# The last LayerNorm over two experts, slot matmuls by four experts, and a new order of the first weights, in a decoder layer with 32 experts

## What is computed

```
x = layernorm(x + self_attention(x))       # 16 heads of 64, biases bq, bk, bv, bo
x = layernorm(x + cross_attention(ctx, x)) # one head of 64, masked keys
x = layernorm(x + moe(x)), with
  probs = softmax(x @ gate.T)              # 32 experts
  topw, topi = top_k(probs, 8); topw /= topw.sum(-1)
  # an expert takes at most 512 tokens (CAPACITY), in order of the tokens
  h   = silu(gate_e(x)) * up_e(x)          # 384 wide
  out = sum over the 8 experts of topw * down_e(h)
```

## Time and profile before

| | |
|---|---|
| time, median of 3 runs | 1892.97 us (1891.65, 1892.97, 2359.14) |
| the profiled execution | 1912.09 us, span 1910.4 us, mean granted clock 0.979 |
| busy: PE, PEld, DVE, ACT, POOL | 94%, 54%, 68%, 60%, 34% of the span |
| rounds | to about 1020 us |
| drain and first slots | to about 1096 us, when expert 0 starts |
| experts | to about 1875 us |
| rest | 35 us |
| moved by DMA | 339.27 MB, mean 178 GB/s |

### The profile page before, as it was taken

One profiled execution on the slowest core, in us unless ns is written; L12 is line 12 of the kernel. 1 busy time (PEld: TensorE's weight loads), 2 busy tenths in 40 slices (PEclk: granted clock), 3 DMA queues, 4 the chain that ended last, 5 costly groups with the idle time before them and its releaser, 6 DMA issues.

```text
span 1910.4 us, 40067 instructions
## 1 busy us (share of the span) xinstructions
PE 1804.4 (94%) x13735; PEld 1040.8 (54%) x13735; DVE 1297.7 (68%) x2695; ACT 1148.8 (60%) x2884; POOL 645.9 (34%) x546
## 2 busy tenths in 40 slices
PE   6899999999999999999999799979999999999992
PEld 3566666667666766666665344434444444444440
DVE  5667989898989898989897674424444444444435
ACT  6877988788878887888787333333333333333325
POOL 1111211121211122111211246545655655555542
PEclk8999999999999999999999999989999999999995
DMA  6647655766466646665568399999999999999968
GB/s 204 155 75 131 141 129 107 158 139 145 96 149 149 143 99 143 151 141 108 131 147 179 118 275 189 214 202 237 250 246 235 233 240 239 242 241 246 216 140 321
DMA packets 596821, 339.27 MB, mean 178 GB/s; under 512 B 492704, under 2 KB 523424, under 8 KB 596768
## 3 DMA queue, kind: packets, MB, share of 16 engines
q1 hardware_dynamic: 567760, 267.28, 61.4%
q0 software_dynamic: 29008, 71.32, 17.7%
HBM read 159.72 MB, written 60.29 MB: 115 GB/s over the span
## 4 chain that ended last, share of the span: by engine, by line
PE 34%; SPq 5%; DMA 4%; DVE 3%; ACT 2%; issue 2%; POOL 1%; POOLq 0%; DVEq 0%; ACTq 0%
PE bank L678 22%; PE bank L1134 10%; SPq L517 4%; DMA arena_v<-arena_p 2%; DMA arena_p<-x_rows,cur_from 1%; PE bank L754 1%; DMA out<-arena_p 1%; DMA stage<-acc_rows 1%; POOL arena_p L2373 0%; PE bank L743 0%; DVE stage L1568 0%; SPq L486 0%; ACT arena_p L1554 0%; ACT stage L1554 0%; POOL acc_rows L2378 0%
## 5 line engine op out<-in xcount | busy, mean ns | idle before, releaser
L2300 POOL TENSOR_TENSOR arena_q<-arena_q 128x512 f16<-128x512 f32 x128 | 166.7, 1303 | 828.7 <-ACT arena_q L1205 721.2
L1568 DVE SCALAR_TENSOR_TENSOR arena_wo<-stage,arena_wo 128x3072 f16<-128x3072 f32 (+3 forms) x78 | 182.4, 2342 | 288.3 <-ACT arena_wo L1313 253.9
L678 PE MATMUL bank<-xt,arena_wo 128*128 128x256 f16 x3072 | 361.4, 275 | 13.1 <-DVE arena_wo L1568 6.9
L678 PEld LDWEIGHTS bank<-xt,arena_wo 128*128 128x128 f16 x3072 | 296.2, 98 | 73.0 <-issue 18.3
L2378 POOL DMA_INDIRECT acc_rows<-arena_wo,cur_to x124 | 203.3, 1639 | 249.6 <-ACT arena_wo L1539 231.3
L678 PE MATMUL bank<-arena_v,arena_wo 128*128 128x512 f16 x1152 | 256.6, 384 | 17.7 <-DMA arena_v<-arena_p 14.6
L1134 PE MATMUL bank<-arena_wo 128*128 128x512 f16 x1152 | 258.2, 383 | 5.4 <-DVE arena_wo L2254 4.6
L678 PE MATMUL bank<-arena_q,arena_wo 128*128 128x512 f16 x1152 | 251.2, 379 | 1.0 <-issue 1.0
L1224 ACT ACTIVATE arena_p<-bank,s_neg 128x256 f32<-128x256 f32 x508 | 234.3, 481 | 29.6 <-DVE s_neg L1604 27.8
L1205 ACT ACTIVATE arena_q<-bank,bqkv 128x256 f32<-128x256 f32 (+1 forms) x512 | 201.7, 485 | 82.4 <-PE bank L678 82.1
L1568 DVE SCALAR_TENSOR_TENSOR stage<-arena_p,s_rden,stage 128x256 f16<-128x256 f32 x508 | 211.7, 478 | 28.3 <-ACT stage L1245 28.3
(11 more groups left out here) (272 smaller groups left out, 2274.1 us busy)
## 6 DMA issues: line engine op xcount, KB each, us to landing
stage<-wguT SPq DMA_DIRECT2D x31, 1536.0 KB
stage<-wdnT SPq DMA_DIRECT2D x32, 768.0 KB, 5.8
xt<-xT SPq DMA_DIRECT2D x16, 512.0 KB, 4.8
xr<-x_rows SPq DMA_DIRECT2D x16, 512.0 KB, 4.1
stage<-ctxT SPq DMA_DIRECT2D x16, 512.0 KB, 3.8
acc_rows<-x SPq DMA_DIRECT2D x15, 512.0 KB, 3.0
x_rows<-stage SPq DMA_DIRECT2D x30, 256.0 KB, 3.7
arena_p<-stage SPq DMA_TRANSPOSE x256, 3.1
```

Of the source, the lines that this page charges most:

```text
L678: mm = pe.matmul(out_ap, lhs(a, i), rhs(c, i), start=(n == 0 and i == 0), stop=(n == 2 and i == chunks - 1))
L1568: return vec.scalar_tensor_tensor(out=dst, in0=src, scalar=scale, in1=hi, op0=ALU.mult, op1=ALU.subtract)
L2300: gp.tensor_tensor(qk[:, j % 2, 1, :], qk32[:, j % 2, :], qk[:, j % 2, 0, :], ALU.subtract).then_inc(qk_lo, 1)
```

## The change

It has four parts.

- **Slots.** In rounds 3 to 15 `fill_slots` uses the form of `fill_rest`: 16 matmuls of 128 x 128 by 128 x 64 for a batch in the place of 64. `add_slots` adds 128 x 512 in the place of 32 x 512. Three small copies on VectorE in the drain (`own_slots`) bring the diagonal blocks together. `bias_rows` has memory of its own, and the index tables move into memory of the context's.
- **Weights in round 0.** `Q2` and `K2` are loaded and split before `V1`. `Q2` takes the place of `K0`, `V1` that of `V0`.
- **First expert.** SP starts the load of expert 1's weights after the first gate product of expert 0, and VectorE does `rest_hots(0)` before its two copies.
- **The last LayerNorm.** The groups are loaded when the scatters of experts 0 to 29 have landed, and their moments, deviations and normalising stand between the steps of experts 30 and 31. Expert 30 isn't scaled on ScalarE or scattered with an addition: GpSimd gathers its rows from `acc_rows`, VectorE adds its result (`fix_sums(0)`), and GpSimd writes the rows back to `acc_rows` after all groups are loaded. Then it gathers expert 31's rows and goes on as before with both sets: over `out`, first those of expert 30, then those of expert 31. TensorE's last `down` waits for `fix_sums(0)`. The memory of the groups is assigned in another order. The last two experts stand outside TensorE's loop.

The diff, cut to its core:

```
-                 [quad(stage[:, 0, 0:GT_ROWS])], [quad(stage[:, 0, GT_ROWS:2 * GT_ROWS])],
-                 [quad(arena_p[:, 0:GT_ROWS])], [quad(arena_v[:, :].bitcast(F32))],
+                 [quad(arena_p[:, 0:GT_ROWS])], [quad(arena_p[:, CC * (D + NX):CC * (D + NX) + GT_ROWS])],
                  [pair_of(x1h[:, :, :].rearrange("p s n -> p (s n)").bitcast(F32)),
                   pair_of(x1T[:, :, :, :, :].rearrange("p s t c n -> p (s t c n)").bitcast(F32))],
-                 [quad(arena_p[:, CC * (D + NX):CC * (D + NX) + GT_ROWS])]]
+                 [quad(stage[:, 0, 0:GT_ROWS])], [quad(stage[:, 0, GT_ROWS:2 * GT_ROWS])],
+                 [quad(arena_v[:, :].bitcast(F32))]]
...
+        LATER = NX - 2
+        fix = [[y[:, 0, c, :] for c in range(CC)], [x1[:, 0, :], x1[:, 1, :], x2[:, 0, :], x2[:, 1, :]]]
...
-        AT = {Q0: 0, K0: 1024, V0: 2048, Q1: 4096, K1: 5120, V1: 0, Q2: 2048, K2: 4096, O0: 0, O1: 2048, X3: 4096, XO: 6144}
-        AFTER = {V1: K0, Q2: V0, K2: K1, O0: V1, O1: Q2, X3: K2}
+        AT = {Q0: 0, K0: 1024, V0: 2048, Q1: 4096, K1: 5120, Q2: 0, V1: 2048, K2: 4096, O0: 0, O1: 2048, X3: 4096, XO: 6144}
+        AFTER = {Q2: K0, V1: V0, K2: K1, O0: Q2, O1: V1, X3: K2}
...
-            for n in (V0, Q1, K1, V1, Q2, K2):
+            for n in (V0, Q1, K1, Q2, K2, V1):
...
-            for c in range(CC):
-                sp.wait_ge(ld_first[c], 16)
             sp.wait_ge(ew_lo_gu, 1)
             sp.wait_ge(ew_lo_dn, 1)
+            sp.wait_ge(g_mm, 1)
             load_expert(1, 0)
...
-            sp.wait_ge(st_y, (NX - 1) * 64)
-            sp.wait_ge(ew_lo_gu, NX)
-            sp.wait_ge(ew_lo_dn, NX)
-            sp.wait_ge(u_mm, (NX - 1) * FC)
+            sp.wait_ge(st_y, LATER * 64)
+            sp.wait_ge(ew_lo_gu, NX - 1)
+            sp.wait_ge(ew_lo_dn, NX - 1)
+            sp.wait_ge(cur_done, 2 * NX - 1)
             for g in range(GROUPS):
+                if g == 5:
+                    sp.wait_ge(ew_lo_gu, NX)
+                    sp.wait_ge(ew_lo_dn, NX)
                 if g == GROUPS - 1:
-                    sp.wait_ge(cur_done, 2 * NX - 1)
+                    sp.wait_ge(u_mm, (LATER + 1) * FC)
                 for n, rows in enumerate(rows3[g]):
...
-                slot_columns(range(NX), True, True).then_inc(slot_mm, 1)
-            def slot_columns(experts, opens, closes):
-                for e in experts:
+                for g in range(NX // ALIKE):
                     for t in range(TT):
-                        mm = pe.matmul(ps_slot[:, e, :], hot_low[:, t * NX + e, :], hot_high[:, t * NX + e, :],
-                                       start=(opens and e == 0 and t == 0), stop=(closes and t == TT - 1),
-                                       skip_group_check=True)
-                return mm
+                        at = slice(t * NX + g * ALIKE, t * NX + (g + 1) * ALIKE)
+                        mm = pe.matmul(ps_alike[:, g, :, :], hot_low[:, at, :], hot_high[:, at, :],
+                                       start=(g == 0 and t == 0), stop=(t == TT - 1), skip_group_check=True)
+                mm.then_inc(slot_mm, 1)
...
-                past(pe, y_done, count(e, CC, -2))
+                if last:
+                    pe.wait_ge(summed, 2)
+                else:
+                    past(pe, y_done, count(e, CC, -2))
...
-                    past(pe, y_done, count(e, CC, c - 3))
+                    if last:
+                        pe.wait_ge(summed, c + 1)
+                    else:
+                        past(pe, y_done, count(e, CC, c - 3))
                     tokens(c, range(FC)).then_inc(y_mm, 1)
...
@@ ScalarE, round 0
                     piece_hi(Q1)
                     piece_hi(K1)
+                    piece_hi(Q2)
...
                     qk_out(b, 2)
+                    if first:
+                        piece_hi(K2)
                     values_hi(b, 1)
-                if first:
-                    piece_hi(V1)
-                    piece_hi(Q2)
...
                     qk_out(b, 4)
+                if first:
+                    piece_hi(V1)
...
@@ ScalarE, experts
+            def normalise(g):
+                act.wait_ge(ln3_rstd, 2 * (g + 1))
+                for t in range(GT):
+                    nc.scalar.activation(row3(g, t), row3(g, t), ACT.Identity, bias=shift3[:, g, t:t + 1],
+                                         scale=rstd3[:, g, t:t + 1]).then_inc(out_done, 1)
+            def normalise_fixed(k):
+                act.wait_ge(fix_rstd, 2 * k + 2)
+                for c in range(CC):
+                    if k == 0 and c == 0:
+                        act.wait_ge(st_fix, 16 * CC)
+                    nc.scalar.activation(fix[k][c], fix[k][c], ACT.Identity, bias=shift4[k][:, c:c + 1],
+                                         scale=rstd4[k][:, c:c + 1]).then_inc(fix_done, 1)
...
-            expert(NX - 2, 0, True, count(NX // 2 - 1, 32, 64))
-            expert(NX - 1, 1, False, 0)
...
+            expert(NX - 2, 0, True, count(NX // 2 - 1, 32, 64), ((), (), (0, 1)))
+            expert(NX - 1, 1, False, 0, ((2,), (3,), (4, 5, 6, 7)))
+            normalise_fixed(0)
+            normalise_fixed(1)
...
@@ VectorE
-                vec.tensor_tensor(slots[0:LOW, :, :], slots[0:LOW, :, :], ps_slot[:, :, :], ALU.add).then_inc(slot_done, 1)
+                vec.tensor_tensor(slots[:, :, :], slots[:, :, :], ps_alike[:, :, :, :].rearrange("p g e h -> p (g e) h"), ALU.add)\
+                   .then_inc(slot_done, 1)
+            def own_slots():
+                own = lambda ap, n: ap.rearrange("p (g e) n -> p g e n", e=ALIKE)[:, :, n, :]
+                dve.wait_ge(slot_done, LAST - 2)
+                for n in range(1, ALIKE):
+                    vec.tensor_copy(own(slots[0:LOW, :, :], n), own(slots[n * LOW:(n + 1) * LOW, :, :], n)).then_inc(slot_done, 1)
...
                     piece_lo(K1)
+                    piece_lo(Q2)
...
+                pair(maxima, 1)
                 if first:
-                    piece_lo(V1)
-                    piece_lo(Q2)
-                pair(maxima, 1)
+                    piece_lo(K2)
...
                 pair(maxima, 3)
+                if first:
+                    piece_lo(V1)
...
                 gate_max(f)
+                own_slots()
                 masked_last(b)
...
+                rest_hots(0)
                 for c in (1, 3):
                     dve.wait_ge(first_mm, c + 1)
                     vec.tensor_copy(xgT[0][:, c].rearrange("p s d n -> p (s d) n"), ps_first[c][:, :, :]).then_inc(first_odd, 1)
-                rest_hots(0)
...
+            def fix_sums(k):
+                dve.wait_ge(ld_fix, (k + 1) * 16 * CC)
+                dve.wait_ge(cur_done, 2 * LATER + 2 + k)
+                for c in range(CC):
+                    dve.wait_ge(y_mm, (LATER + k) * CC + c + 1)
+                    vec.scalar_tensor_tensor(out=fix[k][c], in0=ps_y[c][:, :], scalar=cur_w[:, k, c:c + 1], in1=fix[k][c],
+                                             op0=ALU.mult, op1=ALU.add).then_inc(summed, 1)
...
-                    if not ahead:
-                        group_moments(f)
+                    for g in groups[f]:
+                        group_moments(g)
...
-            expert(NX - 2, 0, True)
-            expert(NX - 1, 1, False)
-            for g in range(FC, GROUPS):
-                group_moments(g)
+            expert(NX - 2, 0, True, ((), (0,), (1, 2)))
+            fix_sums(0)
+            expert(NX - 1, 1, False, ((3,), (4,), (5, 6, 7)))
+            fix_moments(0)
+            fix_sums(1)
             fix_moments(1)
...
@@ GpSimd
-            expert(NX - 2, 0, False, False, 32 * NX - 64)
+            wait_apart(pool, ld_xgt[0], 32 * NX - 64, s_const, N_CONST)
...
+            def gather_fixed(k, chunks):
+                for c in chunks:
+                    gp.indirect_dma_start(fix[k][c], None, acc_rows,
+                                          bass.IndirectOffsetOnAxis(ap=idx_from[:, LATER + k, c:c + 1], axis=0))\
+                      .then_inc(ld_fix, 16)
+            def fixed_rstd(k):
+                pool.wait_ge(fix_ln, FIX_LN * (k + 1))
+                gp.tensor_tensor(rstd4[k][:, :], ve4[k][:, :], neg_half[:, :], ALU.pow).then_inc(fix_rstd, 1)
+                pool.wait_ge(fix_rstd, 2 * k + 1)
+                gp.tensor_tensor(shift4[k][:, :], neg_mean4[k][:, :], rstd4[k][:, :], ALU.mult).then_inc(fix_rstd, 1)
+            def scatter_fixed(k, chunks):
+                for c in chunks:
+                    pool.wait_ge(fix_done, CC * k + c + 1)
+                    gp.indirect_dma_start(out, bass.IndirectOffsetOnAxis(ap=idx_to[:, LATER + k, c:c + 1], axis=0),
+                                          fix[k][c], None).then_inc(st_fix, 16)
+            pool.wait_ge(st_y, LATER * 64)
+            gather_fixed(0, range(CC))
+            for g in range(4):
+                group_rstd(g)
+            for g in range(GROUPS):
```

(30 more changed lines are left out.)

82 lines of the change are left out of this document (37 added, 45 removed).

## The result

Over 20 executions each, the changed kernel takes 1888.19 us in the median (1874.18 to 1909.68) and the kernel before 1893.32. The medians lie 5 us apart where 17.6 were forecast. The ratio is 0.9954 (95% interval 0.9934 to 0.9973); it leaves out the executions more than 1.5% above the fastest of their kernel (1909.68 and 2359.14 here), which count as slow. The profiled execution of the changed kernel took 1876.35 us, 1 us from the predicted 1875. That is the puzzle of this case: one execution does what the sum says, the median doesn't.

The account below looks back on a forecast made before the run. TensorE bounds the experts, TensorE with VectorE close behind the rounds, DMA the last 20 us. Terms of 2.2 + 5.7 + 1.0 + 8.7 = 17.6 us off the 1892.97 median gave 1875.4, predicted as 1875; range 1859 to 1890.

Parts of the forecast that it names:

- round 0: First round: loading and splitting `Q2` and `K2` before `V1` shortens TensorE's waits; 5.7 us, from 1.6 to 8.0.
- last LayerNorm: End of the kernel: groups loaded 23.03 us earlier, beside experts 30 and 31, bring the end forward 8.7 us (3 to 14).
- slots: Rounds 3 to 15: fewer slot matmuls save 1.12 us a round, mostly lost waiting for VectorE; 2.2 us, 0 to 13.4.
- first expert: Expert 0: with expert 1's load later, VectorE's copy of turned tokens may come sooner; 1 us, from −2 to 3.
- I take 0.18 x 12 = 2.2 us: Rounds: only the 0.18 us slack before VectorE's low half of x is gained, in 12 rounds.
- the slow clock behind the wait: Round 0: the `qk_pair` behind the late `K2` would return from 4.39 to 2.78 us, 1.61 us less.
- rival of the late first group: Last LayerNorm: group 0 takes 10.9 us beside four gathers, stalling TensorE; gain 2 instead of 8.7, total 1882; chance 0.14.
- the halving that the prediction drew from the Trainium skill: Last LayerNorm: DMA engines alternate between queues packet by packet, so gathers would halve the first load's rate.
- I infer that the timed runs near the median don't have these waits: Experts 4 and 6: DMA waits explain the 19.1 us between profile (1912.09) and median (1892.97), so the median lacks them.
- slower rival: Experts: expert 1's load, begun 6.5 us later, pushes later loads and brings DMA waits into timed runs; 1901; chance 0.08.
- 10 us of slack cover it: First expert: expert 1's load takes 13.0 us in a 23.03 us period, so starting at most 6.5 us later is harmless.
- The prediction's own sign of being wrong: Experts 2 to 8: waits for DMA at the timed level, listed among the signs that would show the prediction wrong.

Follow-up runs that it names:

- u_round0: The changed kernel with the old order of the first weights in round 0; median 1887.8 us, lowest run 1882.9.
- u_first: The changed kernel with the first expert as before (expert 1's load behind the gathers, `rest_hots(0)` behind the copies); median 1881.65 us.
- u_tail: The changed kernel with the last LayerNorm as before, everything else changed; median 1891.72 us, lowest run 1884.9.
- again2: The changed kernel run once more without any edit; median 1877.52 us over 5 runs, its profiled execution a long one of 1895.69.
- p_first: The changed kernel with expert 4's weights issued behind the transposes of expert 3's tokens; median 1889.22 us, 9 of 12 runs long.
- u_slots: The changed kernel with the old 64 slot matmuls in a round; median 1879.14 us.
- p_late: The changed kernel with each expert's weights issued behind the transposes of the expert before it, a period later; median 1878.44 us.
- after: The changed kernel itself, without further edits, in its first profile; that execution took 1876.35 us.
- w_act: The changed kernel with the weights of experts 3 to 31 started by ScalarE on its own queue; median 1912.27 us.

## Why the prediction was right and where it failed

Two terms of the sum held in mechanism and size, round 0 and the last LayerNorm; the other two were worth nothing:

| term | forecast | measured |
|---|---|---|
| slots | 2.2 (0 to 13.4) | 0 or less (expert 0's start in all traces) |
| round 0 | 5.7 | 5.8 (u_round0, lowest runs), 5.9 (first slot step) |
| first expert | 1 | 0 (u_first; the 0.4 between the lowest runs is inside their spread) |
| last LayerNorm | 8.7 | 7.8 (u_tail), 7.7 (traces) |
| sum | 17.6 | 14.2 and 14.7 (kernels without long runs), 13.8 (traces) |

- **Slots.** The step "I take 0.18 x 12 = 2.2 us" was right in its mechanism and nearly in its size, 0.15 us in each of ten steady rounds. What it left out took this back: 1 us between rounds 3 and 4, and about 1 us between the gathers and expert 0. The chain that sets the round runs through VectorE, which in its turn waits for ScalarE (2.0, 1.5, 0.6 and 0.4 us between 900 and 960 us, the same before and after), and hardly through the slot matmuls.
- **Round 0.** Right in the sum. One sub-term failed, the slow clock behind the wait: the `qk_pair` after the shorter waits still took 4.12 us, which is 0.27 us less and not 1.61. That the sum fits all the same is partly luck: the waits ahead of the three products shrank from 10.81 us to 3.27, by 7.5, where the sum had 6.3 less 2.3 for `V1`.
- **First expert.** The mechanism failed: the copy does come without the 3 us behind "remote", but the last chunk of gathered rows is late next (3.1 us of waits), and expert 0 starts no earlier.
- **Last LayerNorm.** First load 22.5 us earlier relative to expert 30 (23.03 forecast), the stall in `down` 1.37 us (1 forecast), last scatter issue 8.25 us earlier. The rival of the late first group fell: it landed after 5.7 us beside the four gathers. The trace before could have settled this, for it has just this case, which the prediction says it lacks. GpSimd's four gathers of the last expert's rows start there 0.25 us behind the first load, issued at 1851.56:

```profile
1851.81 1.05 POOL L2424 DMA_INDIRECT x<-acc_rows,idx_from  x1 [4.00 <-DMA acc_rows<-arena_wo,cur_to]
```

So what the gathers cost was in the 5.43 us already, and no further lateness was to be expected. Whether the load alone would be faster, as by the halving that the prediction drew from the Trainium skill, no row shows.
- **The step that failed** is the first paragraph's: "I infer that the timed runs near the median don't have these waits", and with it the sum taken off the median of three. For the kernel before it is true near its median, but 26% of its runs are long; of the changed kernel's 49% are, so its median lies at the edge of the long part (1888.19 in the first 20 runs, 12 of them long, and 1882.9 over all 37) and the measured gain was 5 instead of 14. The other 3 us to 17.6 are the slots, the first expert and 1 us of the last LayerNorm. I had three times of before, of which one (2359.14) was an outlier, and a profile 19 us above them; I used the waits only to subtract them and never asked how often they come.
- **The slower rival** named the right place and the right wait, with 0.08. Its mechanism, the moved load of expert 1, is refuted by u_first, and "10 us of slack cover it" treated DMA as a capacity question. What decides is whether weights and transposes overlap in time. The prediction's own sign of being wrong, waits for DMA in experts 2 to 8, came in again2's trace (experts 3 and 5), though not in the first profiled execution.

Why the changed kernel falls into the bad state more often is open. Undoing the first expert, round 0 or the last LayerNorm each leaves 5 or 6 of 12 runs long; undoing the slots gives 5 of 23, and 0 of 6 in p_first's order, which is suggestive and not shown. One difference that reaches the experts is on record, the time from the gathers to expert 0 (up to 13.4 us instead of 11.1 to 11.6); but u_slots's long execution started expert 0 as early as its short ones, so a late start is not needed. The comparisons between sessions also ran on different chips.

## What to carry to other kernels

When a profiled execution lies well above the timed ones, its extra waits are a state that the kernel can fall into: count how often before taking a sum off a median, and look for the loop that keeps it there. Where transposes by DMA and bulk loads share the engines, put the load right behind the transposes, not at the earliest time that its buffer is free; here the earliest time gained nothing and made 1 in 4 to 1 in 2 executions 6 to 33 us longer. An engine 99% busy beside one 92% busy may give back only 0.15 of 1.1 us less work in a round, if the other engine's chain runs back to back ahead of the product that starts the next round. And one pair of traces is not enough to size a part of 1 us: the start of the same stage moved by 3 us between traces of the same code.

## What the runs showed of the hardware

- Four DMA transposes of an expert's tokens take 5.4 to 8.6 us to issue when the last bulk load was issued 13 to 18 us before (p_late), 6.5 to 10.5 us when it was issued 9 to 13 us before (after), and 16.8 to 26.1 us in the stretch of the long execution (again2). With the weights on another queue the same happens in a stretch (w_act: 28.05 us for three of the four). The engines look busier and move less then: DMA share and GB/s from 1140 to 1190 us, short and long execution (columns: window, length, busy us of PE, PEld, DVE, ACT, POOL, PEclk, DMA share, GB/s):

```profile
1140.00:1190.00 50.00, 50.00 (x233) 22.69 (x232) 21.22 (x23) 20.07 (x22) 30.67 (x25) 1.00 1.11 242
```

```profile
1140.00:1190.00 50.00, 39.12 (x171) 17.09 (x170) 18.62 (x19) 14.44 (x15) 24.27 (x22) 0.90 1.18 179
```

- 16 matmuls of 64 columns, each with a new weight tile of 128 x 128, take 0.63 us, 39 ns each, in every round. The Trainium skill (TensorE: Matmul & The Clock Gate, section "Back-to-back issue gap") gives some 81 ns for a pair with 128 columns in a sustained stream; these pairs of half the columns take half of that. No run here has a sustained stream with 128 columns to set beside it.
